# A window-attention and frequency-filter kernel: the opening's pieces go between its scores, and the row's turn and projection ahead of the transposes

## The reference, cut to what matters

```python
freq = abs(dct2(x))                       # per image and channel, 96 x 96
noise_mask = f(freq)                      # one 96 x 96 plane for each image
win = windows of 12 x 12 points           # 64 windows in an image, L = 144
q, k, v = win @ qkv_w.T + qkv_b           # 8 heads of 32 channels
attn = softmax(q @ k.T * SCALE + bias)
out = (attn @ v) @ proj_w.T + proj_b
x_lpe = (conv2d(x, lpe_w, groups=C, pad=1) + lpe_b) * lpe_scale * noise_mask
x_attn_img = out + x_lpe
freq2 = dct2(x_attn_img)
x_freq = idct2(freq2 * sigmoid(5.0 * (abs(freq2) - mean)))
y = batchnorm(conv2d(x + x_freq, fr_w))   # 1 x 1 convolution, statistics over all images
return gelu(y)
```

## Time and profile before

| what | us |
|---|---|
| timed runs | 8455.17, 8457.01, 8464.24 (median 8457.01) |
| the profiled execution | 8434.64, of which span 8432.9 |
| masks, to the end of the stage | 830 |
| one strip in its steady state | 77.3 |
| an opening between two images | 20.6 to 25.2 |
| a tail | 35.0 or 37.9 to 38.8 |
| the frequency stage, an image | 145.8, 150.6 or 158.6 |
| the turn from the frequency stage to z | 19.4 or 20.9 to 21.1 |

### The profile page before, as it was taken

How to read it: one execution, slowest core, us unless ns; L and a number is a source line. 1 busy time by engine, 2 the same in 40 slices (tenths; PEclk the granted TensorE clock), 3 DMA queues, 4 the chain that set the end, 5 groups by cost and what they waited for, 6 DMA issues and landing times.

```text
span 8432.9 us, 251395 instructions
## 1 busy us (share of the span) xinstructions
PE 7852.1 (93%) x84778; PEld 5905.1 (70%) x84778; DVE 5507.1 (65%) x20355; ACT 5152.9 (61%) x17097; POOL 2724.1 (32%) x3673
## 2 busy tenths in 40 slices
PE   9998999999999999999999999999999999999920
PEld 8997676867776777767686777677776777676810
DVE  4555788468855886488747884588648874888410
ACT  5554776457754775377646775577547764776434
POOL 1120443224431443144323443244314431443200
PEclk9999999899999999999999999999999999999965
DMA  7653000110003000200021000200020002000189
GB/s 121 108 97 62 16 22 13 51 59 22 15 16 98 15 22 16 91 16 22 23 68 38 15 16 28 85 22 16 16 91 22 22 16 91 15 22 10 46 355 407
DMA packets 386808, 485.86 MB, mean 58 GB/s; under 512 B 249616, under 2 KB 352528, under 8 KB 369296
## 3 DMA queue, kind: packets, MB, share of 16 engines
q1 hardware_dynamic: 369488, 393.67, 16.2%
q0 software_dynamic: 16192, 77.49, 2.3%
HBM read 319.45 MB, written 151.66 MB: 56 GB/s over the span
## 4 chain that ended last, share of the span: by engine, by line
PE 63%; issue 21%; POOL 9%; DMA 4%; DVE 1%; POOLq 1%; ACT 1%; SPq 0%; DVEq 0%; ACTq 0%
PE ps L983 55%; PE ps L1122 4%; POOL work L441 4%; POOL work L476 3%; DMA AH<-y_scratch 2%; PE ps L1167 2%; DMA out<-AH 2%; PE ps L1119 1%; POOL work L438 1%; PE ps L1120 1%; POOL work L426 1%; POOLq L473 0%; POOL work L432 0%; DVE work L827 0%; ACT AH L685 0%
## 5 line engine op out<-in xcount | busy, mean ns | idle before, releaser
L568 ACT ACTIVATE work<-work 128x144 f32<-128x144 f32 x5120 | 2043.1, 403 | 23.1 <-DVE work L794 13.6
L983 PE MATMUL ps<-work 32*32 32x144 f32 (+3 forms) x32902 | 1711.2, 300 | 68.9 <-issue 30.7
L827 DVE SCALAR_TENSOR_TENSOR work<-xs,lw,work 128x570 f32<-128x570 f32 (+1 forms) x2048 | 1604.8, 820 | 0.0
L794 DVE CUSTOM_DVE_ANT_0 work<-ps,negbias 128x144 f32<-128x144 f32 x5120 | 1246.8, 302 | 494.2 <-issue 407.9
L983 PEld LDWEIGHTS ps<-work 32*32 32x32 f32 (+2 forms) x32902 | 966.9, 127 | 657.8 <-issue 567.2
L438 POOL TENSOR_TENSOR work<-work 128x80 f32<-128x80 f32 x1024 | 471.0, 460 | 2840.0 <-DVE work L801 2827.1
L441 POOL TENSOR_TENSOR work<-work 128x640 f32<-128x640 f32 x1024 | 1286.7, 1257 | 0.0
L983 PE MATMUL ps<-work,wqkv 128*128 128x288 f32 x4096 | 1269.6, 434 | 17.8 <-DVE work L794 11.4
L568 ACT ACTIVATION_READ_ACCUMULATOR work<-work 128x1 f32 x5120 | 971.2, 190 | 0.0
L983 PEld LDWEIGHTS ps<-work,wqkv 128*128 128x128 f32 x4096 | 721.6, 192 | 274.4 <-issue 24.2
L983 PE MATMUL ps<-dct,AH 96*96 96x97 f32 (+1 forms) x7168 | 800.0, 264 | 9.7 <-ACT AH L501 9.2
(11 more groups left out here) (130 smaller groups left out, 11846.4 us busy)
## 6 DMA issues: line engine op xcount, KB each, us to landing
work<-in_x SPq DMA_DIRECT2D x128, 576.0 KB, 5.4
xs<-in_x SPq DMA_DIRECT2D x64, 1152.0 KB, 5.2
AH<-in_x SPq DMA_DIRECT2D x192, 384.0 KB, 3.4
y_scratch<-AH SPq DMA_DIRECT2D x192, 384.0 KB, 2.6
AH<-y_scratch SPq DMA_DIRECT2D x64, 1152.0 KB, 22.8
out<-AH POOLq DMA_DIRECT2D x64, 1152.0 KB, 18.1
xs<-in_x SPq DMA_DIRECT2D x112, 96.0 KB, 5.1
bias_scratch<-in_rpb_rev POOLq DMA_DIRECT2D x144, 4.5 KB, 2.1
```

What stands on the lines that cost most here:

```text
L568: o = act.activation(sp[t % 4][:, c, :], sp[t % 4][:, c, :], ACT.Exp, scale=-1.0, bias=mn[t % 4][:, c:c + 1], accum_out=den[t % 4][:, c:c ...
L794: v.tensor_tensor_reduce(out=sp[t % 4][:, c, :], in0=psS[c], in1=negbias[:, t % 2, c, :], scale=1.0, scalar=BIG, op0=ALU.add, op1=ALU.min, ...
L827: v.scalar_tensor_tensor(dst[:, ct, :, w0:w1], xs[par][:, ct, y0 + dy:y0 + dy + HS, w0 + dx - 1:w1 + dx - 1], lw[:, ct, tap:tap + 1], dst[ ...
L983: return nc.tensor.matmul(o, l, r, start=start, stop=stop)
```

## The change

- In each step of a strip, `row` stands ahead of `transposes`, with its waits. `row` is cut into `turn` and `project`; the wait for the strip's last `o_out` belongs to `project` now.
- In an image's last strip the 36 taps lie in steps 0 to 13, two or three each, none in steps 14 and 15. The second half goes to `xs[0]`, a strip's input that is no longer read (`branch`), in place of a third buffer.
- In the tail the turns of rows 0 and 1 stand ahead of the transposes of step 15, that of row 2 ahead of its `attend`, that of row 3 behind it; only their projections remain in the loop over the 12 rows.
- At the turn to z, the first halves of `zrows(0)` and `zrows(1)` (`zpart`) stand ahead of `i1(62)` and `i1(63)`, the last two groups of the frequency stage.
- In the opening, score 0 follows piece 2, and then come piece 3, piece 4, score 1, piece 5, score 2, piece 6, the wait for score 3, piece 7 and the second half of score 3. Pieces 6 and 7 have banks of their own (`first_banks`), so that head step 0 makes only piece 8. The wait for the last `y` eviction moves behind piece 3 (`freed`). On DVE the statistics of the image before are laid between the evictions of scores 0, 1 and 2, on ACT the copies of the pieces between the exponentials.

The core of the diff:

```diff
-        def pieces_at(t, last):
+        first_banks = (0, 1, 4, 5, 6, 7, 4, 5)
+
+        def pieces_at(t, last, head=False):
...
+            if head and t == 0:
+                return [8]
...
+            if last:
+                return [divmod(k, 18) for k in range(36 * t // 14, 36 * (t + 1) // 14)] if t < 14 else []
...
+        def branch(s, half):
+
+            return xs[0][:, :, 0:HS, :] if s == NS - 1 and half else lpe[(2 * s + half) % 3]
...
 # ACT, opening
+                        piece_out(3)
+                        piece_out(4)
                         exps(0)
+                        piece_out(5)
                         exps(1)
                         piece_out(6)
+                        piece_out(7)
...
 # DVE, opening
-                        for t in range(3):
-                            scores_out(t)
+                        scores_out(0)
+                        beside[0]()
+                        scores_out(1)
                         recip(0)
+                        beside[1]()
+                        scores_out(2)
                         recip(1)
+                        beside[2]()
...
 # PE, opening
-                        pe.wait_ge(S["piece_out"], n * (NP * NPC) + HG)
                         pe.wait_ge(S["q_pad"], b * 6 + 6)
-                        for t in range(3):
-                            before_scores(t)
-                            score(t, signal=False)
-                            few_scores(t).then_inc(S["scores"], 1)
+                        scores_made(0)
+                        piece(3)
+                        freed()
+                        piece(4)
+                        scores_made(1)
+                        piece(5)
+                        scores_made(2)
+                        piece(6)
                         before_scores(3)
-                        piece(6)
+                        piece(7)
                         few_scores(3)
...
 # PE, a step
-                        if head and t == 0:
-                            before_scores(4)
-                        transposes(t)
                         r = None if head else row_at(t)
                         if r is not None:
                             if not (last and t + 3 >= NT):
                                 pe.wait_ge(S["sb_ready"], n * 80 + LC * (t + 3) + psRow + 1)
                             pe.wait_ge(S["a_row"], (n - 1) * WS + r + 1)
                             row(n - 1, r, psRow, 1 - par)
+                        if head and t == 0:
+                            before_scores(4)
+                        if last and t == NT - 1:
+                            pe.wait_ge(S["a_row"], n * WS + 1)
+                            turn(n, 0, 0, par)
+                            turn(n, 1, 1, par)
+                        transposes(t)
...
 # PE, tail
+                        turn(n, 2, 2, par)
                         before_attend(NT - 1)
                         attend(NT - 1)
                         attend_few(NT - 1)
+                        turn(n, 3, 3, par)
...
 # PE, turn to z
-                    if q >= 1:
+                    if 1 <= q < NCH - 1:
                         i1(q - 1)
...
+                zpart(0, 0)
+                i1(NCH - 2)
+                zpart(1, 0)
                 i1(NCH - 1)
```

More of the change, by code:

```diff
@@ L539, in attention, with strip @@
             def attention(b):
-                def strip(s, par, head=False, last=False, first=False, between=((lambda: None),) * NPC):
+                def strip(s, par, head=False, last=False, first=False, between=((lambda: None),) * 3):
                     n = b * NS + s
@@ L545, in piece_out @@
                         p, k = i // NPC, i % NPC
-                        bank = i if i < NPC else psM
+                        bank = first_banks[i] if first else psM
                         act.wait_ge(S["piece"], n * (NP * NPC) + i + 1)
@@ L600, in strip @@
                             o_out(t - 2)
-                        made = pieces_at(t, last)
+                        made = pieces_at(t, last, head)
                         for i in made[:1]:
@@ L783, in attention, with strip @@
             def attention(b):
-                def strip(s, par, head=False, last=False, first=False):
+                def strip(s, par, head=False, last=False, first=False, beside=((lambda: None),) * 3):
                     n = b * NS + s
@@ L820, in lpe_step @@
                             v.wait_ge(S[f"xs_in{par}"], (n - par) * 24 + 48)
+                        if k == 0 and half == 1 and s == NS - 1:
+                            v.wait_ge(S["lpe_step"], n * 36)
                         if tap == 4:
@@ L869, in strip @@
                             scores_out(t + 3)
-                        steps = taps_at(t)
+                        steps = taps_at(t, last)
                         r = None if head else row_at(t)
@@ L939, in image, with last_stats, gathered, kept @@
                 y_stats(NG - 2, 0)
-                y_stats(NG - 1, 1)
-                wait_apart(v, (S["stat"], b * NG + NG))
                 base = b * 7
[L943 to L954, removed]
+                def last_stats():
+                    y_stats(NG - 1, 1)
+                def gathered():
+                    wait_apart(v, (S["stat"], b * NG + NG))
+                    for ct in range(CT):
+                        v.bn_aggr(ag[:, ct, :], stats[:, ct].rearrange("p g s -> p (g s)")).then_inc(S["agg_step"], 1)
+                def kept():
+                    v.wait_ge(S["agg_step"], base + 2)
+                    for ct in range(CT):
+                        dst = agg[:, ct, bass.ds(b, 1), :].rearrange("p b s -> p (b s)")
+                        v.tensor_copy(dst[:, 1:2], ag[:, ct, 0:1]).then_inc(S["agg_step"], 1)
+                        v.tensor_scalar(dst[:, 2:3], ag[:, ct, 1:2], float(HW), None, ALU.mult).then_inc(S["agg_step"], 1)
+                    v.wait_ge(S["agg_step"], base + 6)
+                    v.tensor_copy(ag[:, 0, 0:1], ag[:, 0, 1:2]).then_inc(S["agg_step"], 1)
+                    v.wait_ge(S["agg_step"], base + 7)
+                if ends:
+                    last_stats()
+                    gathered()
+                    kept()
+                else:
+                    attention(b + 1)(0, 0, first=True, beside=(last_stats, gathered, kept))
                 for par in range(2):
@@ L1057, in attention, with strip @@
             def attention(b):
-                def strip(s, par, head=False, last=False, first=False, between=((lambda: None),) * NPC):
+                def strip(s, par, head=False, last=False, first=False, between=((lambda: None),) * 3, freed=lambda: None):
                     n = b * NS + s
@@ L1172, in row, with scores_made @@
                         last.then_inc(S["row_ps"], 1)
+                    def row(m, r, bank, side):
+                        turn(m, r, bank, side)
+                        project(m, r, bank, side)
                     if first:
+                        def scores_made(t):
+                            before_scores(t)
+                            score(t, signal=False)
+                            few_scores(t).then_inc(S["scores"], 1)
                         for i, beside in enumerate(between):
@@ L1264, in image, with zpart @@
                         f2(q + 1)
-                    if q >= 1:
+                    if 1 <= q < NCH - 1:
                         i1(q - 1)
+                def zpart(g, ct):
+                    for i in range(4):
+                        last = mmul(ps[:, 2 * (g % 2) + ct, 96 * i:96 * i + 96],
+                                    xf[ct][:, 4 * g + i, :], inv[:])
+                    return last
+                zpart(0, 0)
+                i1(NCH - 2)
+                zpart(1, 0)
                 i1(NCH - 1)
@@ L1273, in zrows @@
                         pe.wait_ge(S["z_ready"], b * NG + g - 1)
[L1274 to L1277 removed]
+                    for ct in range(1 if g < 2 else 0, CT):
+                        last = zpart(g, ct)
                     last.then_inc(S["zps"], 1)
```

38 lines of the change are left out of this document (18 added, 20 removed).

## The result

The changed kernel takes 8399.5 us (median of 11 runs, 8358.5 to 8423.3) and the kernel before 8454.4 (11 runs, 8440.7 to 8479.3): the ratio is 0.9931, 95% interval 0.9912 to 0.9951. That is 55 us less, where 21 were forecast; it lies in the range. The profiled executions tell it differently: their spans are 8432.9 and 8417.7, only 15 apart. So two questions stand ahead of the others: which stages moved, and why the profile and the timed runs disagree.

What follows compares the result with a forecast made beforehand. PE was taken to bound the kernel, 93% busy, with idle time and half clock at image seams. Opening -47, turn to z -38, steps +54, last strip and tail +10 gave -21: 8436 us, range 8388 to 8492.

Steps and rivals of the forecast that it cites:

- The row ahead: Steps of 48 strips: row ahead of transposes waits for PSUM bank 3, net 1.1 us a strip, +54 us.
- The gain from the earlier addition: Steps of a strip: an earlier row brings its masked addition earlier, removing 0.18 us of stall at the score's fourth head.
- The rival of the full wait: L1167 in every step with a row: wait uncompensated, 2.9 us a strip, +64 in all, 8521 us; chance 0.10.
- the rival of the hidden wait: Steps of a strip: wait mostly hidden, 0.4 us a strip, -55 in all, 8402 us; chance 0.20.
- The opening: Each image's opening: pieces fill PE's waits for score evictions, 16.3 to 16.6 us where it was 24.4; -47 us.
- the time at the loop's start: End of an opening: idle time of PE counted as staying at 1.03 us.
- Score 3 the longest gap: Openings: a sign of being right, with openings of 16 to 19 us; score 3 was to wait 1.5 us.
- The half clock for which 12 us were set aside: Openings: allowance of 12 us for the clock falling again behind the 1.5 us gap at score 3.
- The turn to z: End of frequency stage: z's half groups fill PE's gaps and the clock stays up; -38 us, bounds -9 and -45.
- The tail: Last strip and tail together: +5 for steps, nothing for the end's order, 5 for half clock; +10 us, bounds -15 and +35.
- the replay's "nothing": Tail: replaying the reordered turns and taps gave +0.1 us an image, counted as nothing.
- I add 5 for more of this: Tails: allowance of 5 us for more half clock, seen in 5 of 8 tails, about 3 us each.

Runs made afterwards that it cites:

- filled pair: The kernel before and the changed kernel, each with unread matmuls added in two idle PE places at the frequency stage's start: 8396.4 and 8343.0 us.
- number 9: Changed kernel with two idle PE places filled, DVE evicting each score's fourth head first and PE's row waiting only for that: 8214.3 us, ratio 0.9716.
- filled kernel before: The kernel before with unread matmuls added in two idle PE places at the frequency stage's start: 8396.4 us.
- numbers 11 and 12: The kernel before with two idle PE places filled, plus the whole changed last strip and tail, or its taps alone: 8373.5 and 8380.0 us.

## Why the prediction was right or wrong

**The row ahead: right, and nearly to size.** It said +54, and the profile shows +61. PE's timeline of the changed kernel, in an even step with a short piece (to 3654.83) and an odd one:

```profile
3653.47 1.24 PE L1017 MATMUL ps<-work,wqkv 128*128 128x288 f32 x4
3654.83 0.42 PE L1201 MATMUL ps<-eye,work 128*96 128x128 f32 x2
...
3659.20 1.24 PE L1017 MATMUL ps<-work,wqkv 128*128 128x288 f32 x4
3660.49 0.42 PE L1201 MATMUL ps<-eye,work 128*96 128x128 f32 x2
```

DVE's fourth eviction in the odd step:

```profile
3660.35 0.08 DVE L808 DVE_READ_ACCUMULATOR2_ANT work<- 128x1 f32 x1
```

The turn starts 1.36 and 1.29 us after its piece, where 1.07 is the piece's own time: waits of 0.29 and 0.22. In the odd step it is 0.06 after the eviction's end (3660.43), as the prediction had read it in the tail. The prediction had 0.47 and 0.24. The gain from the earlier addition is 1.2 us a strip by number 9, where it had 1.8. The wait was put at 2.9 a strip and cost 2.4, the gain at 1.8 and brought 1.2. The two errors nearly cancel in the difference, 1.1 forecast and 1.2 to 1.3 measured, and that they do so is luck. (48 strips of 1.1 are 53; the 54 is a slip of one.) The rival of the full wait has its place right, and without the gain its price would have been 2.4; it falls. So does the rival of the hidden wait, though its -55 and 8402 are what was measured: the time alone would have pointed at the wrong cause, the strips of 78.5 don't.

**The opening: the sum right, the working not.** It said -47; the profiled pair gives -45, the filled pair -50, of which 4 are lost again in the first strips. PE's waits in an opening of the changed kernel:

```profile
4451.23 0.91 PE L1017 MATMUL ps<-work 32*128 32x144 f32 x16 [0.40 <-DVE work L808]
...
4454.20 1.23 PE L1017 MATMUL ps<-work,wqkv 128*128 128x288 f32 x4 [0.91 <-DVE work L808]
...
4458.44 0.86 PE L1017 MATMUL ps<-work 32*128 32x144 f32 x8 [2.63 <-issue]
```

Score 2 waits 0.40 and score 3 0.91, where it had 0.55 and 1.5. But the time at the loop's start is 2.63, where it took the 1.03 of the kernel before as fixed. That is the term that was mis-sized: 2.3 to 2.6 us in the six openings ahead of the loop's jump back. "Score 3 the longest gap" fails with it.

What is nearly fixed there is another time: from the first matmul behind the opening's last wait to the first one behind the jump it is 3.7 to 4.3 us in the kernel before and 3.9 to 4.2 in the changed one. In both, and in all six openings, a 16 KB packet of the queue that brings instructions starts 1.1 to 1.2 us into that time, takes 1.0 to 1.6, and the first matmul comes 1.5 to 1.7 after it. In the changed kernel, from 4454.20 to 4458.40 us (DMA queue and kind; packets, MB, share of 16 engines):

```profile
q8 instruction: 1, 0.02, 2.1%
```

The last image's code stands behind the loop, with no jump; its opening has no such packet and no idle time at this place, in either kernel. So the traces say that PE waits for code there, and that the code is fetched only after the last wait. The kernel before had 2.9 us of matmuls to do meanwhile, at half clock; the changed one has 1.6, at the full clock. Moving that last wait earlier was not tried.

The half clock for which 12 us were set aside came behind that gap and not behind score 3: 3 to 7 us at 0.50 in each of the six openings that have the gap, 37 in all, or some 18 lost by halving (an estimate); none in the opening that doesn't have it, though the waits of 0.40 and 0.91 stand there too. The six other profiled kernels with this opening show the same.

**The turn to z: right in kind, under-sized.** -44 in the profiled pair and -50 in the filled one, forecast -38. The -50 lies outside its own bound of -45. It set aside one or two images in which the clock falls as before; in none of the eight does it. And it took 6.80 us of half clock an image, where the filled kernel before has 10 in seven images and 14 in one. It also put all four waits on L908 an image at this turn; one of the four, the longest (up to 1.7), is the second gap at the stage's start, which the change leaves alone: of the 16 that remain in the changed kernel (two an image) one is that.

**The tail: wrong in sign.** +10 was forecast for last strip and tail; it is -15, and -20 in the filled pair. The last strips' +6.8 was foreseen (+5). Two terms failed. One is the replay's "nothing", +0.1 an image: where the clock doesn't fall in it, a tail takes 35.0 us before and 33.7 after, some 10 us less in eight. The other is "I add 5 for more of this": half clock in the tails was to become more frequent, and it became rarer and shorter (7 to 10 us in five of eight tails before, some 3 in four after; in the filled pair in six and in one). That makes the other 11 us in the profiled pair and 16 in the filled one. The replay had the waits of steps 11 to 15 in it, but set the gain of the vanished wait for POOL against new waits of about the same length, and gave the clock a price without asking which of them lie close together. The waits at the last transposes are now one of 1.5 an image (12.0 in 8), where they were three on DVE and one on POOL, 3.7 together; against them stand two waits of 1.2 on L1201, which lie steps ahead of it. That the clock fell because the old waits lay close together is an argument; what numbers 11 and 12 show is that it falls less often without them.

**What was not in the sum: the frequency stage.** Having put that gap at the wrong end of the stage, the prediction had no term for the clock behind it, and it carried the profiled execution's difference to the median over unchanged. That was an error of method. The kernel before, profiled, has the highest granted clock that its runs show (0.955 at 8434.6; other runs go to 0.950 at 8473), and the changed kernel, profiled, the lowest (0.962 at 8419.3; others to 0.971 at 8358.5). Which images lose their clock behind the two gaps, and for how long, changes from run to run. At the medians it cancels: filling the gaps takes 56 us from the kernel before and 57 from the changed one, so the missing term isn't why the forecast was small. With the gaps filled the runs of a kernel lie within 5 to 11 us of each other and the change is worth -53. That is the figure to hold against the forecast of -21: by the stages, whose sum is -56, some 30 of the 35 between them are the tail's (-20 for +10) and 12 the turn's, less 7 for the steps; the openings with the strips behind them came out as forecast. The direction was right for reasons that mostly held; that the size still lay in the range owes something to the opening's and the steps' errors, which cancel.

## What to carry to other kernels

A wait moved ahead costs its lateness at the new place, and here PE, which goes through its program in order, showed it; before giving the move up, look at whether the awaited result can be made first, since here one changed order of evictions turned +1.2 us a strip into -1.2. Where the granted clock varies between runs, a seam's idle time can be paid for in the stage behind it: here filling two gaps made the comparison sharp as well as each kernel 56 to 83 us faster. And a gap that stands ahead of a loop's jump need not shrink with the work around it: look at what it is counted from.

## What the hardware showed that was not expected

After the two gaps at the start of the frequency stage the clock stayed at 0.50 for long although PE was busy all the time; in one image of the changed kernel:

```profile
4181.35:4218.80 37.45, 37.45 (x181) 31.12 (x180) 9.78 (x27) 12.99 (x36) 7.42 (x9) 0.50 0.09 34
```

Half clock in the tails lasted 3 to 10 us. The Trainium skill, page "TensorE: Matmul & The Clock Gate", section "What's actually happening", says that activity releases the throttle; here 37.45 us of matmuls without idle time in the profile's sense did not, while the same matmuls behind ten added ones kept the clock at 1.00 from the start. Why it stays low so long in some images is open.

The idle time at the start of the loop over images, 2.63 us where it was 1.03 with the same instructions behind the jump, is counted from the last wait ahead of it, as the packets of instructions above show; the list of waits has no releaser for it.
